# Routing logits of seven batches moved into the last batch of the first cross attention

## The chip, the cores and the metric

The kernel runs on one core of a Trainium2 chip. A core has a matrix engine (TensorE, PE in the profile, with its weight loads as PEld), a vector engine (VectorE, DVE), an activation engine (ScalarE, ACT), GpSimd (POOL) and SyncE (SP), which here only issues transfers. Each engine runs its own instruction queue in order, and queues meet at semaphores. SBUF is the working memory, PSUM the memory into which PE writes. The metric is the device time of one execution in microseconds (us); lower is better.

## What is computed

Two decoder layers over x of shape (8, 256, 256), 2048 tokens of 256 values. Each layer is: x = layernorm(x + attention(x)), x = layernorm(x + cross_attention(x, context)), x = layernorm(x + ffn(x)). The first layer's attention is windowed, its feed-forward part is a mixture of experts; the second has a gated recurrence, another cross attention and a feed-forward part with binary weights. The part around the change is this:

```python
# first cross attention: 16 heads of 16, 77 context rows per batch
scores = jnp.einsum('bhqd,bhkd->bhqk', Q, K) / np.sqrt(D_K)
...
x = _layernorm(x + _L0_xattn_ref(...))
# routing
logits = tokens @ router_w.T            # 2048 x 256 by 256 x 8
probs = jax.nn.softmax(logits, axis=-1)
top1_idx = jnp.argmax(probs, axis=-1)
top1_prob = jnp.max(probs, axis=-1)
order = jnp.lexsort((-top1_prob, top1_idx))
...
keep = jnp.zeros((T,), bool).at[order].set(keep_sorted)   # capacity 320 per expert
return jnp.where(keep, top1_idx, 0)
```

The order of tokens by probability needs the logits of all 2048 tokens, so nothing of it can start before the last token's logits are there.

## The kernel before

The stages run one after another, each in a block of its own that ends with a barrier of all engines: window attention, cross attention 0, routing and experts, recurrence, cross attention 1, binary feed-forward. The tokens stay in SBUF as `X` (the trace's `tokens`): 16 tiles of 128 tokens, two tiles per batch.

**Cross attention** (`cross_attention`, from L996) goes through 8 batches; the first and the last are written out, the six between are a loop. A batch has 8 units c = 0 to 7 of four heads each (4 units per token tile). Of a unit, PE turns the probabilities into PSUM (`turn_probs`, L1280), ACT takes their fp16 high part (`pth`, L1146), DVE the rest (`ptl`, L1186), and PE multiplies both with the values (`weigh`, L1294). ACT also makes the exponentials (L1138), POOL subtracts the maximum (L1090). The scores of two units lie in the two PSUM banks `s_banks`; from unit 5 of the last batch on nobody needs them any more. Between units stand, on two shared banks, `heads` (transposes of a tile's output `o`, L1251), ACT's copy `ot` (L1131) and `mix` (output projection, L1256), then on DVE the residual (L1203), the statistics (L145 to L150), a root on POOL (L155) and the norm's `apply` (L159), which writes the tile into `X` and counts `ln_done`. In the last batch tile 0 gets heads and mix in units 6 and 7; for tile 1 they stand in an epilogue behind unit 7, and with them a `normalise` (L1193, L1197) and the last `apply`. The queues there hold, in order:

```python
# vector                                   # tensor
both(batch)(dve)                           both(batch)(pe)
norm.apply(dve, BATCH - 1, 0, ...)         weigh(BATCH - 1, UNITS - 1, 1)
normalise(BATCH - 1, 1)                    heads, then mix (epilogue)
residual(BATCH - 1, 1, ...)
norm.apply(dve, BATCH - 1, 1, ...)
```

**Routing** (`route`, from L1371) opens by making the logits in 8 pairs of tiles, one pair per batch. Of a pair, PE turns the tokens with 4 transposes into one of two PSUM banks (L1643), ACT copies them as fp16 `xh` (L1520), DVE makes the fp16 rest `xl` (L1561), and PE makes 12 small matmuls, high x high, high x low and low x high, with 8 columns each into `l_bank` (L1471). The router's weights are loaded first in this block (L1480) and split the same way (L1515, L1557). Buffers are two, so a pair waits for the one two before it. When all are there, DVE takes `best`, the maximum per token (L1566), and `gap`; keys, ranks and slots follow (slot at L1629), then sixteen indirect DMAs by POOL write the tokens into their slots (L1508). SP issues the loads of the first experts' weights and of later stages at the start of this block (L1716 on). The experts then start with transposes of the gathered rows (L1928).

## Time and profile before

| | us |
|---|---|
| time, median of 3 runs | 1263.29 (1261.61 to 1265.4) |
| the profiled execution | 1262.5 |
| its span in the trace | 1260.8 |
| PE busy | 1073.7 (85%) |
| DVE busy | 959.5 (76%) |
| ACT busy | 692.8 (55%) |
| POOL busy | 385.3 (31%) |

The profile is one execution, taken by the hardware profiler. Its times count from the start of the span. An instruction's row gives its start, its duration, engine, line, operation and tiles; in square brackets stands how long its engine sat idle before it and what ended that. The granted clock is TensorE's, as a share of 2.4 GHz.

### The profile page before, as it was taken

How to read it: one execution, taken by the hardware profiler on the slowest of the kernel's cores; microseconds unless marked ns; L12 is line 12 of the kernel's file. 1: busy time of each engine (PE TensorE's matmuls, PEld its weight loads, DVE VectorE, ACT ScalarE, POOL GpSimd, SP SyncE). 2: the span in 40 equal slices, each digit the busy share in tenths (PEclk: the TensorE clock that was granted, in tenths of full speed). 3: DMA queues.
4: the chain of work that ended last, by engine and by line, in shares of the span. 5: the costliest groups of instructions: out<-in, count | busy, mean ns of one | idle time of the engine just before them, and what ended most of it. 6: DMA issues, size and time to landing. Idle time of an engine off the chain costs nothing. (4 is left out here: it accounts for less than half of the span.)

```text
span 1260.8 us, 30092 instructions
## 1 busy us (share of the span) xinstructions
PE 1073.7 (85%) x10763; PEld 858.9 (68%) x10763; DVE 959.5 (76%) x2126; ACT 692.8 (55%) x1459; POOL 385.3 (31%) x538
## 2 busy tenths in 40 slices
PE   5899989999998799975279999389999769998696
PEld 3578878878877577764267777377788647776485
DVE  7687878878877588984838883569998659898397
ACT  2454444444555355543637775368777725555484
POOL 5122222222221356640220000523421325665132
PEclk9899999999999899995569999699999969999799
DMA  7000000200000410007235431300000000000011
GB/s 261 7 10 2 11 12 2 83 3 2 2 2 2 162 42 22 19 1 292 74 113 176 175 117 43 123 17 18 30 12 20 1 14 23 22 11 9 35 51 50
DMA packets 34072, 65.34 MB, mean 52 GB/s; under 512 B 7591, under 2 KB 23335, under 8 KB 30887
## 3 DMA queue, kind: packets, MB, share of 16 engines
q1 hardware_dynamic: 32422, 59.62, 13.5%
q0 software_dynamic: 1536, 4.20, 1.0%
q8 instruction: 73, 1.20, 0.4%
q14 instruction: 41, 0.33, 0.1%
HBM read 43.03 MB, written 12.39 MB: 44 GB/s over the span
## 5 line engine op out<-in xcount | busy, mean ns | idle before, releaser
L1146 ACT ACTIVATE ca_pth<-ca_turned 77x512 f16<-77x512 f32 x128 | 75.9, 593 | 102.8 <-PE ca_turned L1280 102.8
L395 ACT ACTIVATE wa_probs<-wa_scores,wa_minus_top 128x192 f32<-128x192 f32 x256 | 83.3, 437 | 80.7 <-DVE wa_minus_top L488 80.7
L1090 POOL TENSOR_TENSOR ca_z<-ca_z,ca_top 128x308 f32<-128x308 f32 x128 | 88.1, 700 | 113.5 <-DVE ca_top L1181 113.4
L1186 DVE SCALAR_TENSOR_TENSOR ca_ptl<-ca_turned,ca_pth 77x512 f16<-77x512 f32 x128 | 87.1, 680 | 23.0 <-ACT ca_pth L1146 23.0
L351 POOL TENSOR_TENSOR wa_q<-wa_by_cos,wa_by_sin 128x256 f32<-128x256 f32 x32 | 23.4, 730 | 265.4 <-DVE wa_by_sin L483 265.4
L1280 PE MATMUL ca_turned<-ident,ca_probs 128*77 128x128 f32 x512 | 87.1, 294 | 15.1 <-ACT ca_probs L1138 15.0
L406 ACT ACTIVATE wa_pth<-wa_turned 128x384 f16<-128x384 f32 x128 | 58.4, 506 | 72.3 <-PE wa_turned L715 72.3
L1280 PEld LDWEIGHTS ca_turned<-ident,ca_probs 128*77 128x77 f32 x512 | 57.3, 151 | 46.0 <-ACT ca_probs L1138 26.1
L640 PE MATMUL wa_scores<-wa_xh,wa_wh 128*128 128x256 f16 x256 | 71.0, 277 | 10.1 <-DVE wa_wl L467 8.8
L488 DVE TENSOR_REDUCE wa_minus_top<-wa_scores 128x2 f32<-128x384 f32 x128 | 62.3, 548 | 20.8 <-PE wa_scores L703 18.9
L715 PE MATMUL wa_turned<-ident,wa_probs 128*128 128x128 f32 x512 | 68.3, 275 | 7.8 <-ACT wa_probs L395 3.9
L640 PE MATMUL wa_scores<-wa_xl,wa_wh 128*128 128x256 f16 x256 | 71.1, 278 | 0.0
L640 PE MATMUL wa_scores<-wa_xh,wa_wl 128*128 128x256 f16 x256 | 71.0, 277 | 0.0
L1138 ACT ACTIVATE ca_probs<-ca_z 128x308 f32<-128x308 f32 x128 | 57.7, 451 | 23.2 <-POOL ca_z L1090 23.2
L536 DVE SCALAR_TENSOR_TENSOR wa_ptl<-wa_turned,wa_pth 128x384 f16<-128x384 f32 x128 | 64.9, 548 | 6.6 <-ACT wa_pth L406 6.6
L2472 PE MATMUL re_g<-re_convh,re_w_gh 128*128 128x256 f16 x256 | 69.8, 273 | 0.0
L2472 PE MATMUL re_g<-re_convl,re_w_gh 128*128 128x256 f16 x256 | 69.8, 273 | 0.0
L2472 PE MATMUL re_g<-re_convh,re_w_gl 128*128 128x256 f16 x256 | 69.8, 273 | 0.0
L2456 PE MATMUL re_in<-re_xt,re_w_in 128*128 128x256 f32 x256 | 61.6, 402 | 9.0 <-ACT re_xt L2225 9.0
L715 PEld LDWEIGHTS wa_turned<-ident,wa_probs 128*128 128x128 f32 x512 | 57.4, 141 | 15.1 <-issue 6.2
L2456 PEld LDWEIGHTS re_in<-re_xt,re_w_in 128*128 128x128 f32 x256 | 50.9, 202 | 18.8 <-issue 7.2
L1903 DVE SCALAR_TENSOR_TENSOR ex_hl<-ex_h,ex_hh 128x320 f16<-128x320 f32 x72 | 35.2, 488 | 37.3 <-ACT ex_h L1875 36.4
(356 smaller groups left out, 3654.8 us busy)
## 6 DMA issues: line engine op xcount, KB each, us to landing
ex_stage<-in_ew SPq DMA_DIRECT2D x16, 1024.0 KB, 6.9
slots<-slots_zeros SPq DMA_DIRECT2D x10, 512.0 KB, 6.2
ca_xs<-tokens SPq DMA_DIRECT2D x16, 256.0 KB, 2.4
ex_xe<-slots SPq DMA_DIRECT2D x11, 320.0 KB, 3.2
slots<-ex_y SPq DMA_DIRECT2D x9, 320.0 KB
wa_x_stage<-in_xt SPq DMA_DIRECT2D x8, 256.0 KB, 3.1
tokens<-in_x SPq DMA_DIRECT2D x1, 2048.0 KB, 15.3
ca_w<-in_xw SPq DMA_DIRECT2D x2, 1024.0 KB, 6.6
```

What stands on the lines that cost most here:

```text
L395: ins = act.activation(probs[2 * (u % 2) + t][:, h, t * WINDOW:t * WINDOW + SPAN], s_bank[i][:, t * SPAN:(t + 1) * SPAN], ACT.Exp, bias=mi ...
L406: act.activation(spans(pth[k][:]), spans(t_bank[h][:]), ACT.Copy, scale=PSCALE).then_inc(probs_high, 1)
L488: dve.tensor_reduce(minus_top[:, g % 2, i], s_bank[i][:, 0:2 * SPAN].rearrange("p (t s) -> p t s", t=2), AX.X, ALU.max, negate=True).then_ ...
L536: dve.scalar_tensor_tensor(out=spans(ptl[k][:]), in0=spans(t_bank[h][:]), scalar=PSCALE, in1=spans(pth[k][:]), op0=ALU.mult, op1=ALU.subtr ...
L640: ins = pe.matmul(bank[:, a * SEQ:(a + 1) * SEQ], weight[:, k, cols], x[:, par, k], start=(m == 0), stop=(m == 3 * KT_ - 1))
L715: ins = pe.transpose(t_bank[h][:, j * SEQ + t * P:j * SEQ + (t + 1) * P], probs[2 * (u % 2) + t][:, h, j * P:(j + 1) * P], ident[:])
L1090: pool.tensor_tensor(z[k][:, heads], z[k][:, heads], top[:, k, heads].unsqueeze(2).broadcast_to((P, UH, CTX)), ALU.subtract).then_inc(shif ...
L1146: act.activation(pth[k][0:CTX], t_bank[k][0:CTX], ACT.Copy, scale=PSCALE).then_inc(probs_high, 1)
L1186: dve.scalar_tensor_tensor(out=ptl[k][0:CTX], in0=t_bank[k][0:CTX], scalar=PSCALE, in1=pth[k][0:CTX], op0=ALU.mult, op1=ALU.subtract).then ...
L1280: ins = pe.transpose(t_bank[k][0:CTX, h * P:(h + 1) * P], probs[k][:, h], ident[:])
L2456: ins = pe.matmul(i_bank[s % 2][:, k], w_in[:, g, m * P:(m + 1) * P], xt[:, g], start=(g == 0), stop=(g == KT_ - 1))
L2472: ins = pe.matmul(g_bank[m][:, k], w[:, j, cols], x[par][:, j], start=(n == 0), stop=(n == 3 * HT - 1))
```

## The change

The logits of pairs 0 to 6 are made inside the last batch of the first cross attention, pair 7 alone in the routing. A new class `RouteStart` holds the router's weights, the fp16 buffers, the semaphores and a table `logit` in SBUF, and tells for each engine which step stands at which place of the last batch: on PE behind units 5, 6 and 7, behind the last `weigh`, behind heads and behind mix; on ACT behind units 5, 6 and 7 and at the end; on DVE at the head of units 6 and 7's `ptl`, ahead of tile 0's apply, behind the last normalise (ahead of the last residual) and behind the last statistics (ahead of the last apply). The turned tokens go into the two banks of scores, the logits into `o_bank[0]`, the output bank of tile 0. ACT copies the logits from PSUM into `logit`, 14 tiles at the end of the attention and 2 in the routing; DVE reads them from there. The router's load stands in the attention's SP queue. The second cross attention gets a `Nothing`, whose steps are empty.

```diff
@@ cross_attention @@
+class Nothing:
...
-def cross_attention(nc, start, ctx_dram, ident, half, X, next_loads=None, table=None):
+def cross_attention(nc, start, ctx_dram, ident, half, X, follow, next_loads=None, table=None):
+        spare = [s_banks[:, UH * k:UH * (k + 1)].rearrange("p (g t) q -> p g (t q)", g=KT_) for k in range(2)]
+        turned = [bank[:].rearrange("p (g t) -> p g t", g=KT_) for bank in t_bank]
         norm = Norm(ctx, nc, tag, half)
+        follow.add_buffers(ctx, nc, tag + "next_")
         token_sum = sem("token_sum")
         scores = sem("scores")
         masked = sem("masked")
@@ -1064,6 +1089,7 @@
             start.stage(sp, X, 1, 1)
             if next_loads:
                 next_loads(sp)
+            follow.load(sp)
             if table:
                 table.fill(sp)
 
@@ -1118,6 +1144,7 @@
                 table.prepare(pool)
             both(batch)(pool)
             norm.root(pool, BATCH - 1, 1)
+            follow.gpsimd(pool, X)
 
         @block.scalar
         def _(act):
@@ -1153,11 +1180,14 @@
                         step(b + d, (par + d) % 2, kind, i, bank, uses)
                     if c == 2 and after:
                         start.value_high(act, b + 1, 1 - par)
+                    if c >= 5 and not after:
+                        follow.scalar(act, c, spare, turned, o_bank[0])
 
             power(0, 0)
             both(batch)(act)
             for kind, i, bank, uses in CA.epilogue():
                 step(BATCH - 1, 1, kind, i, bank, uses)
+            follow.scalar(act, "last", spare, turned, o_bank[0])
 
         @block.vector
         def _(dve):
@@ -1210,6 +1240,8 @@
                     if two_on and c % 2 == 0:
                         mask_scores(*two_on)
                         take_maximum(*two_on)
+                    if c >= 6 and not after:
+                        follow.vector(dve, c, spare)
                     if c == 5:
                         normalise(b, 0)
                     if c == 1 and before:
@@ -1230,11 +1262,14 @@
             mask_scores(0, 0)
             take_maximum(0, 0)
             both(batch)(dve)
+            follow.vector(dve, "applied", spare)
             norm.apply(dve, BATCH - 1, 0, at(X, (BATCH - 1) * TPB))
             normalise(BATCH - 1, 1)
+            follow.vector(dve, "normalised", spare)
             for kind, i, bank, uses in CA.epilogue():
                 if kind == "mix":
                     residual(BATCH - 1, i, bank, uses)
+            follow.vector(dve, "summed", spare)
             norm.apply(dve, BATCH - 1, 1, at(X, (BATCH - 1) * TPB + 1))
 
         @block.tensor
@@ -1309,13 +1344,19 @@
                         score_pair(b, c + 3, par)
                     if c in (5, 7) and after:
                         score_pair(b + 1, c - 5, 1 - par)
+                    if c >= 5 and not after:
+                        if c == 5:
+                            pe.wait_ge(masked, PAIRS * BATCH)
+                        follow.tensor(pe, c, X, norm, spare, turned, o_bank[0], ident)
 
             score_pair(0, 0, 0)
             score_pair(0, 2, 0)
             both(batch)(pe)
             weigh(BATCH - 1, UNITS - 1, 1)
+            follow.tensor(pe, "weighed", X, norm, spare, turned, o_bank[0], ident)
             for kind, i, bank, uses in CA.epilogue():
                 step(BATCH - 1, 1, kind, i, bank, uses)
+                follow.tensor(pe, kind, X, norm, spare, turned, o_bank[0], ident)
 
         block_scope.close()
         nc.clear_and_free_semaphores(sems + start.sems)
@@ new class, and route @@
+class RouteStart:
+    TURNS = {5: (0, 1), 6: (2,), 7: (3,), "weighed": (4,), "heads": (5,), "mix": (6,)}
+    LOGITS = {6: (0,), 7: (1,), "weighed": (2,), "heads": (3,), "mix": (4, 5, 6)}
+    HIGHS = {5: (0, 1), 6: (2,), 7: (3, 4), "last": (5, 6)}
+    LOWS = {6: (0, 1), 7: (2,), "applied": (3,), "normalised": (4, 5), "summed": (6,)}
+    EARLY = BATCH - 1
+    def __init__(self, ctx, nc, router_dram):
+        def sb(name, shape, dt=F32):
+            return ctx.enter_context(nc.sbuf_tensor("rt_" + name, shape, dt))
+        def sem(name):
+            return ctx.enter_context(nc.semaphore("rt_" + name))
+        self.router_dram = router_dram
+        self.router = sb("router", [P, KT_, EXPERTS])
+        self.router_h = sb("router_h", [P, KT_, EXPERTS], F16)
+        self.router_l = sb("router_l", [P, KT_, EXPERTS], F16)
+        self.logit = sb("logit", [P, TILES, EXPERTS])
+        self.router_loaded = sem("router_loaded")
+        self.router_high = sem("router_high")
+        self.router_low = sem("router_low")
+        self.x_turned = sem("x_turned")
+        self.x_high = sem("x_high")
+        self.x_low = sem("x_low")
+        self.logits = sem("logits")
+        self.kept = sem("logits_kept")
+    def add_buffers(self, ctx, nc, tag):
+        def sb(name):
+            return ctx.enter_context(nc.sbuf_tensor(tag + name, [P, KT_, 2 * P], F16))
+        self.xh = [sb(f"xh{k}") for k in range(2)]
+        self.xl = [sb(f"xl{k}") for k in range(2)]
+    def turn(self, pe, j, X, bank, ident):
+        if j >= 2:
+            pe.wait_ge(self.x_low, j - 1)
+        for t in range(2):
+            for g in range(KT_):
+                ins = pe.transpose(bank[:, g, t * P:(t + 1) * P], X[:, 2 * j + t, g * P:(g + 1) * P], ident[:])
+        ins.then_inc(self.x_turned, 1)
+    def multiply(self, pe, j, out, at_tile):
+        pe.wait_ge(self.x_low, j + 1)
+        pe.wait_ge(self.router_low, 1)
+        for t in range(2):
+            n = 0
+            for g in range(KT_):
+                for x, w in ((self.xh, self.router_h), (self.xh, self.router_l), (self.xl, self.router_h)):
+                    ins = pe.matmul(out[:, at_tile + t, 0:EXPERTS], x[j % 2][:, g, t * P:(t + 1) * P], w[:, g],
+                                    start=(n == 0), stop=(n == 3 * KT_ - 1))
+                    n += 1
+        ins.then_inc(self.logits, 1)
+    def high(self, act, j, bank):
+        act.wait_ge(self.x_turned, j + 1)
+        if j >= 2:
+            act.wait_ge(self.logits, j - 1)
+        act.activation(self.xh[j % 2][:], bank, ACT.Copy, scale=SCALE).then_inc(self.x_high, 1)
+    def low(self, dve, j, bank):
+        dve.wait_ge(self.x_high, j + 1)
+        dve.scalar_tensor_tensor(out=self.xl[j % 2][:], in0=bank, scalar=SCALE, in1=self.xh[j % 2][:],
+                                 op0=ALU.mult, op1=ALU.subtract).then_inc(self.x_low, 1)
+    def keep(self, act, pairs, out):
+        act.wait_ge(self.logits, pairs.stop)
+        act.activation(self.logit[:, 2 * pairs.start:2 * pairs.stop], out, ACT.Copy).then_inc(self.kept, 1)
+    def load(self, sp):
+        sp.dma_start(self.router[:], self.router_dram).then_inc(self.router_loaded, 16)
+    def gpsimd(self, pool, X):
+        pass
+    def scalar(self, act, place, spare, turned, out):
+        if place == 5:
+            act.wait_ge(self.router_loaded, 16)
+            act.activation(self.router_h[:], self.router[:], ACT.Copy, scale=SCALE).then_inc(self.router_high, 1)
+        for j in self.HIGHS.get(place, ()):
+            self.high(act, j, spare[j % 2])
+        if place == "last":
+            self.keep(act, slice(0, self.EARLY), out[:, 0:2 * self.EARLY, 0:EXPERTS])
+    def vector(self, dve, place, spare):
+        if place == 6:
+            dve.wait_ge(self.router_high, 1)
+            dve.scalar_tensor_tensor(out=self.router_l[:], in0=self.router[:], scalar=SCALE, in1=self.router_h[:],
+                                     op0=ALU.mult, op1=ALU.subtract).then_inc(self.router_low, 1)
+        for j in self.LOWS.get(place, ()):
+            self.low(dve, j, spare[j % 2])
+    def tensor(self, pe, place, X, norm, spare, turned, out, ident):
+        for j in self.LOGITS.get(place, ())[:1]:
+            if j == 0:
+                pe.wait_ge(norm.ln_done, (BATCH - 1) * TPB)
+            self.multiply(pe, j, out, 2 * j)
+        for j in self.TURNS.get(place, ()):
+            pe.wait_ge(norm.ln_done, (j + 1) * TPB)
+            self.turn(pe, j, X, spare[j % 2], ident)
+        for j in self.LOGITS.get(place, ())[1:]:
+            self.multiply(pe, j, out, 2 * j)
+def route(nc, opening, slots, ident, X, slot, starts, ahead_of_experts, binary):
 
 
     with ExitStack() as ctx:
@@ -1379,7 +1530,6 @@
         def sem(name):
             return ctx.enter_context(nc.semaphore("rt_" + name))
 
...
-        x_bank = [ctx.enter_context(nc.psum_tensor(f"rt_x{k}", [P, KT_, 2 * P], F32)) for k in range(2)]
-        l_bank = ctx.enter_context(nc.psum_tensor("rt_logit_bank", [P, TILES, 32], F32))
+        x_bank = ctx.enter_context(nc.psum_tensor("rt_x", [P, KT_, 2 * P], F32))
+        l_bank = ctx.enter_context(nc.psum_tensor("rt_logit_bank", [P, 2, 32], F32))
...
+        late = opening.EARLY
...
-            sp.dma_start(router[:], router_dram).then_inc(router_loaded, 16)
...
-            act.wait_ge(router_loaded, 16)
-            act.activation(router_h[:], router[:], ACT.Copy, scale=SCALE).then_inc(router_high, 1)
-            for j in range(TILES // 2):
-                act.wait_ge(x_turned, j + 1)
-                if j >= 2:
-                    act.wait_ge(logits, j - 1)
-                act.activation(xh[j % 2][:], x_bank[j % 2][:], ACT.Copy, scale=SCALE).then_inc(x_high, 1)
+            opening.high(act, late, x_bank[:])
+            opening.keep(act, slice(late, BATCH), l_bank[:, :, 0:EXPERTS])
             act.wait_ge(gap_ready, 1)
...
-            dve.wait_ge(router_high, 1)
-            dve.scalar_tensor_tensor(out=router_l[:], in0=router[:], scalar=SCALE, in1=router_h[:],
-                                     op0=ALU.mult, op1=ALU.subtract).then_inc(router_low, 1)
-            for j in range(TILES // 2):
-                dve.wait_ge(x_high, j + 1)
-                dve.scalar_tensor_tensor(out=xl[j % 2][:], in0=x_bank[j % 2][:], scalar=SCALE, in1=xh[j % 2][:],
-                                         op0=ALU.mult, op1=ALU.subtract).then_inc(x_low, 1)
+            opening.low(dve, late, x_bank[:])
             dve.wait_ge(consts, 13)
-            dve.wait_ge(logits, TILES // 2)
-            l = l_bank[:, :, 0:EXPERTS]
+            dve.wait_ge(opening.kept, 2)
+            l = opening.logit[:]
             then(dve.tensor_reduce(best[:], l, AX.X, ALU.max))
...
-            for j in range(TILES // 2):
-                if j >= 2:
-                    pe.wait_ge(x_low, j - 1)
-                for t in range(2):
-                    for g in range(KT_):
-                        ins = pe.transpose(x_bank[j % 2][:, g, t * P:(t + 1) * P], X[:, 2 * j + t, g * P:(g + 1) * P], ident[:])
-                ins.then_inc(x_turned, 1)
-                if j:
-                    logit(pe, j - 1)
-            logit(pe, TILES // 2 - 1)
+            opening.turn(pe, late, X, x_bank, ident)
+            opening.multiply(pe, late, l_bank, 0)
...
+        opening = RouteStart(ctx, nc, ins["router"])
-            cross_attention(nc, start0, ins["context"], ident, half, X, table=slots)
+            cross_attention(nc, start0, ins["context"], ident, half, X, opening, table=slots)
-        cross_attention(nc, start1, ins["context"], ident, half, X)
+        cross_attention(nc, start1, ins["context"], ident, half, X, Nothing())
```

## Rows read from the trace of the kernel before

**Rows 1.** The page's head: length of the profiled span.

```profile
span 1260.8 us, 30092 instructions
```

**Rows 2.** Windows: start:end, us, busy (instructions) of PE, PEld, DVE, ACT, POOL, clock, DMA share, GB/s.

```profile
560.00:565.00 5.00, 3.66 (x56) 3.09 (x56) 3.29 (x8) 2.75 (x6) 3.03 (x5) 1.00 0.01 3
565.00:570.00 5.00, 1.91 (x16) 1.36 (x15) 1.90 (x8) 0.38 (x1) 0.55 (x1) 0.73 0.00 0
570.00:575.00 5.00, 1.54 (x5) 0.77 (x4) 1.59 (x6) 0.00 (x0) 1.00 (x4) 0.50 0.00 0
575.00:580.00 5.00, 3.00 (x32) 2.54 (x31) 1.46 (x3) 1.19 (x3) 1.53 (x12) 0.50 0.74 257
580.00:585.00 5.00, 4.69 (x61) 3.67 (x58) 2.33 (x4) 2.39 (x4) 0.00 (x0) 0.50 1.01 426
585.00:590.00 5.00, 2.90 (x44) 2.10 (x42) 2.76 (x7) 1.50 (x3) 0.00 (x0) 0.50 1.01 415
...
600.00:610.00 10.00, 3.21 (x90) 2.79 (x90) 10.00 (x11) 9.90 (x8) 0.00 (x0) 0.50 0.15 59
```

**Rows 3.** Timeline: start us, us, engine, line; end of attention, opening of routing.

```profile
573.12 0.41 DVE L159 TENSOR_SCALAR tokens<-ca_res,ca_mv,ca_rstd 128x256 f32<-128x256 f32 x1 [0.66 <-POOL ca_rstd L155]
...
574.59 1.94 PE L1643 MATMUL rt_x<-ident,tokens 128*128 128x128 f32 x8 [3.46 <-PEq L1322]
...
577.05 0.22 ACT L1515 ACTIVATE rt_router_h<-rt_router 128x16 f16<-128x16 f32 x1 [8.11 <-DMA rt_router<-in_router]
...
588.94 0.29 DVE L1566 TENSOR_REDUCE rt_best<-rt_logit_bank 128x16 f32<-128x128 f32 x1 [0.65 <-PE rt_logit_bank L1471]
```

**Rows 4.** Timeline of the routing: POOL's last constant; steps of the last pair.

```profile
576.33 0.13 POOL L1502 IOTA rt_steps<- 128x7 f32 x1
...
585.84 1.09 PE L1643 MATMUL rt_x<-ident,tokens 128*128 128x128 f32 x4
...
586.97 0.60 ACT L1520 ACTIVATE rt_xh<-rt_x 128x512 f16<-128x512 f32 x1 [0.67 <-PE rt_x L1643]
...
587.60 0.69 DVE L1561 SCALAR_TENSOR_TENSOR rt_xl<-rt_x,rt_xh 128x512 f16<-128x512 f32 x1 [0.57 <-ACT rt_xh L1520]
...
588.34 0.19 PE L1471 MATMUL rt_logit_bank<-rt_router_h,rt_xh 128*128 128x8 f16 x1 [0.78 <-DVE rt_xl L1561]
...
588.66 0.17 PE L1471 MATMUL rt_logit_bank<-rt_router_h,rt_xl 128*128 128x8 f16 x1
```

**Rows 5.** Timeline of the attention: transposes at full clock, then the last batch.

```profile
518.68 0.66 PE L963 MATMUL ca_shared<-ident,ca_xs 128*128 128x128 f32 x4
...
562.43 0.69 DVE L1186 SCALAR_TENSOR_TENSOR ca_ptl<-ca_turned,ca_pth 77x512 f16<-77x512 f32 x1 [0.67 <-ACT ca_pth L1146]
...
563.30 1.03 PE L1256 MATMUL ca_shared<-ca_w,ca_ot 128*128 128x256 f32 x4
...
563.50 0.59 ACT L1146 ACTIVATE ca_pth<-ca_turned 77x512 f16<-77x512 f32 x1 [0.48 <-PE ca_turned L1280]
...
566.68 0.41 DVE L159 TENSOR_SCALAR tokens<-ca_res,ca_mv,ca_rstd 128x256 f32<-128x256 f32 x1 [0.66 <-POOL ca_rstd L155]
...
567.29 0.42 DVE L1197 TENSOR_TENSOR ca_o<-ca_out,ca_inv 128x256 f32<-128x256 f32 x1
...
567.86 0.66 PE L1251 MATMUL ca_shared<-ident,ca_o 128*128 128x128 f32 x2 [2.53 <-DVE ca_o L1197]
...
569.09 2.04 PE L1256 MATMUL ca_shared<-ca_w,ca_ot 128*128 128x256 f32 x4 [0.56 <-ACT ca_ot L1131]
...
571.17 0.42 DVE L1203 TENSOR_TENSOR ca_res<-ca_shared,ca_xb 128x256 f32<-128x256 f32 x1 [3.45 <-PE ca_shared L1256]
```

**Rows 6.** Timeline behind the routing: slots, scatter, the experts' first transposes.

```profile
619.18 0.17 DVE L1629 TENSOR_TENSOR slot<-rt_place,rt_place_side 128x16 int32<-128x16 f32 x1
...
620.34 1.24 POOL L1508 DMA_INDIRECT slots<-tokens,slot  x1 [43.73 <-DVE slot L1629]
...
648.64 1.33 PE L1928 MATMUL ex_turned<-ident,ex_xe 80*128 80x80 f32 x8 [4.94 <-DMA ex_xe<-slots]
```

More of the change, by code:

```diff
@@ L1368, in wait_filled, with add_buffers, load, gpsimd @@
         engine.wait_ge(self.zeroed, 16 * FILLS)
-def route(nc, router_dram, slots, ident, X, slot, starts, ahead_of_experts, binary):
+class RouteStart:
[22 more added lines that the diff above has]
+        self.kept = sem("logits_kept")
+    def add_buffers(self, ctx, nc, tag):
+        def sb(name):
[32 more added lines that the diff above has]
+        act.activation(self.logit[:, 2 * pairs.start:2 * pairs.stop], out, ACT.Copy).then_inc(self.kept, 1)
+    def load(self, sp):
+        sp.dma_start(self.router[:], self.router_dram).then_inc(self.router_loaded, 16)
+    def gpsimd(self, pool, X):
+        pass
+    def scalar(self, act, place, spare, turned, out):
+        if place == 5:
[5 more added lines that the diff above has]
+            self.keep(act, slice(0, self.EARLY), out[:, 0:2 * self.EARLY, 0:EXPERTS])
+    def vector(self, dve, place, spare):
+        if place == 6:
[4 more added lines that the diff above has]
+            self.low(dve, j, spare[j % 2])
+    def tensor(self, pe, place, X, norm, spare, turned, out, ident):
+        for j in self.LOGITS.get(place, ())[:1]:
[7 more added lines that the diff above has]
+            self.multiply(pe, j, out, 2 * j)
@@ L1380, in sem @@
             return ctx.enter_context(nc.semaphore("rt_" + name))
-        router = sb("router", [P, KT_, EXPERTS])
         before = sb("before", [P, P])
@@ L1392, in route @@
         plus_half = sb("plus_half", [P, 1])
-        router_h = sb("router_h", [P, KT_, EXPERTS], F16)
-        router_l = sb("router_l", [P, KT_, EXPERTS], F16)
-        xh = [sb(f"xh{k}", [P, KT_, 2 * P], F16) for k in range(2)]
-        xl = [sb(f"xl{k}", [P, KT_, 2 * P], F16) for k in range(2)]
+        opening.add_buffers(ctx, nc, "rt_late_")
         gap = sb("gap", [P, TILES, EXPERTS])
@@ L1461, in route @@
         scattered = sem("scattered")
-        def logit(pe, j):
-            pe.wait_ge(x_low, j + 1)
-            pe.wait_ge(router_low, 1)
-            for t in range(2):
-                n = 0
-                for g in range(KT_):
-                    for x, w in ((xh, router_h), (xh, router_l), (xl, router_h)):
-                        ins = pe.matmul(l_bank[:, 2 * j + t, 0:EXPERTS], x[j % 2][:, g, t * P:(t + 1) * P], w[:, g],
-                                        start=(n == 0), stop=(n == 3 * KT_ - 1))
-                        n += 1
-            ins.then_inc(logits, 1)
+        late = opening.EARLY
         block = ctx.enter_context(nc.Block())
@@ L1683, in _, with experts @@
             binary.add_sizes(pe, k_bank)
-def experts(nc, router_dram, w1_dram, w2_dram, bias_dram, slots, slot, ident, X, next_loads, gates, binary):
+def experts(nc, opening, w1_dram, w2_dram, bias_dram, slots, slot, ident, X, next_loads, gates, binary):
     with ExitStack() as ctx:
@@ L1769, in first_high2 @@
             gates.power_of_base(act)
-        route(nc, router_dram, slots, ident, X, slot, starts,
+        route(nc, opening, slots, ident, X, slot, starts,
               {"sync": first_loads, "vector": first_split, "scalar": first_high2}, binary)
@@ L2849, in ahead_loads @@
             then_loads(sp)
-        experts(nc, ins["router"], ins["ew1"], ins["ew2"], ins["eb"], slots, slot, ident, X, ahead_loads, gates, binary)
+        experts(nc, opening, ins["ew1"], ins["ew2"], ins["eb"], slots, slot, ident, X, ahead_loads, gates, binary)
         cross1 = CrossWeights(ctx, nc, "ca1", additive=True)
```

14 lines of the change are left out of this document (5 added, 9 removed).

## The prediction

> **What bounds the kernel now.** I read the page first: a span of 1260.8 us in one profiled execution of 1262.5, so 1.7 us lie outside the span [rows 1]. No engine's share decides here; the stretch between two stages does. So I went to the busy time by windows around the end of the first cross attention and the opening of the routing [rows 2]. Up to 565 the engines are busy; from 565 to 575, the epilogue of the attention, PE works 1.91 and 1.54 us of 5, DVE 1.90 and 1.59, ACT 0.38 and 0. From 575 to 590 the routing makes logits: PE is well occupied but at a granted clock of 0.50 (the 1.2 GHz level), DVE and ACT are half empty. Nothing in that stretch runs beside the logits but loads.
>
> The timeline of the opening [rows 3] gives its length. The last token tile is normalised by 573.12 + 0.41 = 573.53; the barrier takes until 574.59, when PE's first transpose starts; the first thing that needs all logits, the maximum `best`, starts at 588.94. That is 14.35 us from first transpose to `best`. ACT meanwhile waits 8.11 us for the router's weights, until 577.05, so the first two pairs of tiles are late as well.
>
> What follows `best` hangs on it in one line: the slots at 619.18, which POOL awaited for 43.73 us, sixteen indirect DMAs from 620.34, and the experts' first transposes at 648.64, which waited for the gathered rows [rows 6]. So a microsecond won at `best` should be one won at the end, unless something not moved with it becomes late.
>
> **What the change takes out of the routing.** Seven of eight pairs go, with the router's load and split. The eighth stays, and its steps are those of the last pair now [rows 4]: transposes to ACT 586.97 - 585.84 = 1.13; ACT to DVE 0.63; DVE to the first logit matmul 588.34 - 587.60 = 0.74; twelve matmuls 588.66 + 0.17 - 588.34 = 0.49; on to the next engine 588.94 - 588.83 = 0.11. New is the copy of the logits out of PSUM by ACT (128x16). The trace has no such copy; its nearest row is the router's split on ACT, 0.22 us for 128x16 [rows 3], plus some 0.03 for DVE to see it; the logit wait of 0.11 stands already in the sum. Bounds are 0 and the 0.60 of a 128x512 copy; I take 0.25. Sum 1.13 + 0.63 + 0.74 + 0.49 + 0.11 + 0.25 = 3.35 us. POOL's constants are no new limit: the last of them starts at 576.33 [rows 4], 1.74 us after the start, below 3.35. The routing becomes 14.35 - 3.35 = **11.0 us** shorter. The router's 8 KB load goes into the attention's SP queue, a batch loop earlier; there it stands ahead of the slots' zero fill and nobody waits for either.
>
> **What it puts into the last batch.** Per pair, in work: four transposes (0.66 us at full clock, 1.09 at half [rows 5, 4]), one ACT copy 0.60, one DVE subtraction 0.69, twelve matmuls 0.49. Seven pairs are 4.2 us of ACT, 4.8 of DVE, and 8 to 11 of PE. I walked the queues in program order.
>
> Units 5 and 6: eight transposes stand ahead of the turning of unit 6's probabilities, at 561.1 now; at full clock, 0.13 each (a third of 0.66 less 0.27 for the last), they free PE at about 561.6, 0.5 late. On DVE the two subtractions stand ahead of unit 6's `ptl`, which waited 0.67 us for ACT at 562.43 [rows 5]; it ends 0.7 late. Unit 7's copy, at 563.50, comes 0.65 late, and `ptl` after it. The mix of tile 0 (563.30) starts 0.65 late, and then `weigh` of unit 7 stands behind the logits of pair 1 and the transposes of pair 3.
>
> Between the batch and the epilogue: the subtraction of pair 3 stands ahead of the norm's apply at 566.68. It waits for ACT's copy of pair 3 at about 566.2 to 566.8, ends at 567.5, then come the apply and `o`, at 568.1 instead of 567.29. **First term: +0.8 us.**
>
> Epilogue: heads at 568.7 instead of 567.86. Behind them on PE now stand the logits of pair 3 and the transposes of pair 5, ahead of the mix. Only ACT's copy of the heads, 569.09 - 567.86 = 1.23 with the transposes, covers them. At half clock: 568.7 + 0.5 (heads) + 0.35 (issue of twelve matmuls, 588.34 to 588.66 [rows 4]) + 0.95 (four transposes, 1.09 less the drain of the last) = 570.5 to 570.6 against 569.09: 1.5 late, of which 0.8 was there. **Second term: +0.7.** The subtractions of pairs 4 and 5 stand ahead of the residual on DVE, but pair 5's ends near 572.0 and the mix (2.04 us at half clock [rows 5]) at 572.65, so the mix hides them; without that cover they would cost 0.7 each.
>
> After the mix: now 573.53 - 571.17 = 2.36 us from the residual to the last apply. The new chain beside it: logits of pair 4 (0.35 to issue, 0.15 of it before the mix has ended), transposes of pair 6 1.13, copy 0.63, subtraction 0.74, logits of pair 6 0.49, copy 0.11 + 0.22. From the mix's end that is 3.5 to 3.6. **Third term: +1.2.** The statistics and POOL's root run beside it.
>
> Together +2.7 at half clock. Bounds: nothing below 0, since no step of the epilogue becomes shorter at the same clock; above, see the rivals.
>
> **The clock** is the largest open point. In the trace it stands at 1.00 from 560 to 565, 0.73 on average from 565 to 570 and 0.50 after [rows 2]; PE had then done little. Heads and mix so ran at the 1.2 GHz level (0.66 and 2.04 us, against 1.03 for the mix of tile 0 [rows 5]). The added work fills those idle times, which could hold the clock up. But the same work in the routing did not raise it: 580 to 585 has PE busy 4.69 of 5 us at 0.50 [rows 2]. I take it that the clock falls where it fell.
>
> The Trainium skill bears on this (TensorE: Matmul & The Clock Gate, Part 4: PE-mode transpose): transposes do not count as a busy PE for the clock gate. The row of 580 to 585 agrees with it. Its Part 1 on what the gate does says that activity releases the throttle; by that alone the second rival's time below, 1252.7, would come.
>
> **Sum.** 11.0 - 2.7 = 8.3 us. 1262.5 - 8.3 = 1254.2; the median of the three runs is 0.8 above the profiled execution, so 1255.0. Downstream nothing is changed. The bulk loads occupy the DMA engines fully until shortly after 600 and hardly from 600 to 610 (share 0.15) [rows 2]; the slots would be ready at 611 and the scatter starts then, clear of them.
>
> **Rivals.**
> 1. *As forecast*, 1255.0, its own range 1253 to 1257: chance 0.50.
> 2. *The clock holds through the epilogue.* Heads, transposes and mix take about half: mix ends 571.0, then DVE's statistics at 572.5, subtraction of pair 6 by 573.2, logits and copy by 574.0 against 573.53: cost 0.5 instead of 2.7, 1252.7. For: PE's idle time of 2.53 us before the heads [rows 5] shrinks. Against: the 580 to 585 row. Chance 0.20.
> 3. *The clock falls earlier*, since the mix of tile 0 comes later and transposes fill the time before it. Then that mix takes 1.0 us more and the transposes of pair 3 0.43 more ahead of unit 7's `weigh`: about +1.6, cost 4.3, 1256.6. Chance 0.20.
> 4. *Slower than before.* ACT and DVE take their queues in order, so each copy and subtraction that waits for PE holds the attention's own steps. If the rounds of all seven pairs fell in series on that path, each is 1.13 + 0.63 + 0.74 + 0.49 = 2.99 us at half clock, 20.9 together against 11.0 won: +9.9, 1273. It decides from 3.7 exposed rounds on. For: steps are placed one beside another with no slack. Against: the idle time in 565 to 575 [rows 2], and my walk exposes less than one. Chance 0.03.
> 5. *Nothing is won at the end*: routing is shorter, but a load or a conversion for the experts is late. Then 1262 to 1264. Against: the loads are done 10 us before the slots, and all conversions before the experts follow the slots on DVE. Chance 0.07.
>
> **Chances and range.** A difference under 0.3% (3.8 us) is what a measurement of this kernel can't tell from none. Rivals 1 to 3 lie beyond it (0.90, 6.7 us at least); so faster 0.90, same 0.06, slower 0.04, with rival 5 leaning to same and a little to both sides. The range takes in rivals 1 to 3 and the 2 us by which the three runs stand off their median: 1250.8 to 1259.0.
>
> **What would show it.** After the change `best` starts some 3.3 us after the first transpose of the routing; that transpose starts 2.7 us later than 574.59; the second mix starts 1.5 us later; slots near 611; the experts' first transposes near 640.3. The prediction is wrong if the first transpose comes over 5 us later, if the copy of the logits takes over 1 us, or if slots and experts' transposes move by different amounts.

## The result, and the profile after the change

The changed kernel takes 1253.41 us (median of 4 runs, 1252.91 to 1253.86) against 1263.72 for the kernel before on the same chip: ratio 0.9923, 95% interval 0.9911 to 0.9936, that is 9.7 us faster (8.1 to 11.2). Its profiled span is 1251.9 us, against 1260.8 [rows 1].

The windows of the same stretch as in [rows 2], with the same columns:

```profile
560.00:565.00 5.00, 4.05 (x61) 3.75 (x62) 4.90 (x11) 3.96 (x11) 3.44 (x5) 1.00 0.01 3
565.00:570.00 5.00, 3.47 (x64) 3.05 (x63) 4.27 (x13) 2.19 (x4) 0.55 (x1) 1.00 0.00 0
570.00:575.00 5.00, 3.47 (x62) 3.08 (x61) 3.12 (x9) 1.80 (x4) 0.55 (x1) 1.00 0.02 5
575.00:580.00 5.00, 1.57 (x16) 1.12 (x16) 1.27 (x3) 0.82 (x3) 1.98 (x14) 0.55 0.58 205
580.00:585.00 5.00, 3.78 (x17) 3.41 (x17) 2.95 (x14) 2.67 (x5) 0.00 (x0) 0.50 1.01 426
```

The clock is the difference to look for. It stood at 0.73 and 0.50 from 565 to 575; now it is 1.00 in both windows, and falls at about 575.5, in the barrier. PE's busy time there went from 3.45 us to 6.94, DVE's from 3.49 to 7.39.

The end of the attention and the opening of the routing, in order of time (start, duration, engine; idle before in brackets):

```profile
569.31 0.42 DVE L1227 TENSOR_TENSOR ca_o<-ca_out,ca_inv 128x256 f32<-128x256 f32 x1
...
569.88 0.41 PE L1286 MATMUL ca_shared<-ident,ca_o 128*128 128x128 f32 x2 [1.53 <-DVE ca_o L1227]
...
570.43 0.64 PE L1454 MATMUL ca_scores<-ident,tokens 128*128 128x128 f32 x4
570.90 1.05 PE L1291 MATMUL ca_shared<-ca_w,ca_ot 128*128 128x256 f32 x4
...
572.34 0.41 DVE L1233 TENSOR_TENSOR ca_res<-ca_shared,ca_xb 128x256 f32<-128x256 f32 x1
...
573.54 0.68 DVE L1478 SCALAR_TENSOR_TENSOR ca0next_xl<-ca_scores,ca0next_xh 128x512 f16<-128x512 f32 x1
...
574.29 0.41 DVE L159 TENSOR_SCALAR tokens<-ca_res,ca_mv,ca_rstd 128x256 f32<-128x256 f32 x1
...
574.77 0.26 ACT L1484 ACTIVATE rt_logit<-ca_out 128x112 f32<-128x112 f32 x1 [1.41 <-PE ca_out L1465]
...
576.07 1.09 PE L1454 MATMUL rt_x<-ident,tokens 128*128 128x128 f32 x4 [1.34 <-PEq L1363]
...
577.20 0.60 ACT L1474 ACTIVATE rt_late_xh<-rt_x 128x512 f16<-128x512 f32 x1 [2.16 <-PE rt_x L1454]
...
579.10 0.18 ACT L1484 ACTIVATE rt_logit<-rt_logit_bank 128x16 f32<-128x16 f32 x1 [1.30 <-PE rt_logit_bank L1465]
...
579.39 0.28 DVE L1682 TENSOR_REDUCE rt_best<-rt_logit 128x16 f32<-128x128 f32 x1 [0.87 <-ACT rt_logit L1484]
```

The two transposes of the heads now take 0.41 us and the epilogue's mix 1.05; they took 0.66 and 2.04 [rows 5]. On DVE the subtraction of pair 6 (573.54) runs between statistics and apply, and ACT's copy of 14 tiles of logits is the last thing, 0.33 us behind the apply's end. The routing then has one pair; from first transpose (576.07) to `best` (579.39) are 3.32 us instead of 14.35 [rows 3].

What hangs on it, to hold against [rows 6]:

```profile
609.63 0.18 DVE L1745 TENSOR_TENSOR slot<-rt_place,rt_place_side 128x16 int32<-128x16 f32 x1
...
610.79 1.24 POOL L1635 DMA_INDIRECT slots<-tokens,slot  x1 [32.70 <-DVE slot L1745]
...
639.17 1.33 PE L2036 MATMUL ex_turned<-ident,ex_xe 80*128 80x80 f32 x8 [4.71 <-DMA ex_xe<-slots]
```

Slots and the experts' first transposes come 9.55 and 9.47 us earlier: nothing in between became late. The last batch itself began 1.3 us later in this execution than in the one before (unit 4's copy on ACT at 559.71 against 558.42), with the same code ahead of it. So positions are compared below by distances inside the stretch: **the stretch** runs from ACT's copy of unit 5's probabilities to the routing's first transpose (14.47 us before; 14.67 after, the 14.65 of the expectations being taken to PE's weight load), **the opening** from there to `best`.

### The profile page after: what moved, and what is told of

Its sections match the earlier page's. It is cut to its first block and busy times, and to the rows that moved or that the text cites. A ratio compares the mean times of both kernels' runs of the same rounds, so it can differ in the third digit from the quotient of the medians.

```text
span 1251.9 us, 30100 instructions
## 1 busy us (share of the span) xinstructions
PE 1069.3 (85%) x10763; PEld 856.2 (68%) x10763; DVE 958.7 (77%) x2126; ACT 693.1 (55%) x1461; POOL 385.7 (31%) x538
## 5 line engine op out<-in xcount | busy, mean ns | idle before, releaser
L640 PE MATMUL wa_scores<-wa_xh,wa_wh 128*128 128x256 f16 x256 | 70.4, 275 | 11.2 <-DVE wa_wl L467 9.1
```

The source lines that it names most:

```text
L640: ins = pe.matmul(bank[:, a * SEQ:(a + 1) * SEQ], weight[:, k, cols], x[:, par, k], start=(m == 0), stop=(m == 3 * KT_ - 1))
```

## Experiments

All are compared with the kernel before on the same chip. Two edits serve several of them: in "route as before" the routing has a `RouteStart` of its own with `EARLY = 0`, which loads and splits the router and makes all eight pairs, and `best` reads `l_bank` in PSUM. In the table, mix 0 is the one of tile 0, heads and mix 1 those of the epilogue. "Last fall" is the moment at which the granted clock fell to 0.50 for the rest of the attention, worked out from windows of 0.5 us and counted from the start of the epilogue's heads (minus: before them). e9 and e10 are single executions (1261.98 and 1261.31 us) and have no ratio; in e8 and e12 no transpose opens the routing, so they have no stretch and no opening.

| run | mix 0 | heads | mix 1 | last fall | stretch | opening | ratio (95%) |
|---|---|---|---|---|---|---|---|
| before | 1.03 | 0.66 | 2.04 | -0.6 | 14.47 | 14.35 | |
| after | 1.03 | 0.41 | 1.05 | +5.6 | 14.67 | 3.32 | 0.9923 (0.9911 to 0.9936) |
| e1 before again | 1.03 | 0.66 | 2.04 | -0.5 | 14.48 | 14.07 | 0.9999 (0.9988 to 1.0010) |
| e2 cost alone | 1.03 | 0.41 | 1.05 | +5.2 | 15.09 | 13.69 | 1.0001 (0.9991 to 1.0011) |
| e3 transposes only | 1.03 | 0.41 | 1.10 | +6.2 | 13.49 | 14.07 | 0.9999 (0.9990 to 1.0009) |
| e10 the same again | 1.03 | 0.41 | 2.05 | +7.3 | 14.95 | 14.05 | |
| e4 small matmuls only | 1.03 | 0.66 | 2.05 | -0.5 | 14.49 | 14.05 | 1.0011 (1.0002 to 1.0021) |
| e5 router early | 1.91 | 0.66 | 2.05 | -8.3 | 15.93 | 12.92 | 0.9998 (0.9988 to 1.0009) |
| e9 the same again | 1.03 | 0.66 | 2.05 | -0.5 | 14.50 | 12.91 | |
| e6 four pairs | 1.03 | 0.41 | 1.10 | +2.1 | 14.04 | 7.46 | 0.9951 (0.9935 to 0.9968) |
| e7 all at the end | 1.03 | 0.66 | 2.05 | -0.5 | 23.68 | 3.31 | 0.9979 (0.9969 to 0.9988) |
| e11 after again | 1.03 | 0.41 | 1.05 | +5.1 | 16.27 | 3.31 | 0.9922 (0.9910 to 0.9935) |
| e8 last pair too | 1.03 | 0.41 | 1.05 | +5.6 | | | 0.9899 (0.9882 to 0.9916) |
| e12 the same again | 1.03 | 0.41 | 1.05 | +5.2 | | | 0.9894 (0.9880 to 0.9907) |

**e1, the kernel before once more.** No edit.

> The unchanged kernel, for a second trace. The stretch asked about goes from ACT's copy of unit 5's probabilities in the last batch to the first transpose of the routing: 14.47 us before the change (560.12 to 574.59), 14.65 after it (561.40 to 576.05), though seven pairs were added. Theory A (the added PE work held TensorE's clock at 1.00 through the epilogue, which paid for the queueing): here the clock falls to 0.50 before the epilogue's mix again and the stretch is 14.5 again, give or take 0.5. Theory B (where the clock falls is chance, the trace of before caught a bad case): the stretch comes out near 13.2, with the mix near 1.03 us instead of 2.04. Ratio 1.000 under both.

PE in its epilogue:

```profile
570.63 0.66 PE L1251 MATMUL ca_shared<-ident,ca_o 128*128 128x128 f32 x2 [2.53 <-DVE ca_o L1197]
...
571.85 2.04 PE L1256 MATMUL ca_shared<-ca_w,ca_ot 128*128 128x256 f32 x4 [0.56 <-ACT ca_ot L1131]
```

The fall is no accident of the first trace: heads 0.66 and mix 2.04 again, stretch 14.48. Theory B falls for the epilogue. Where it falls, windows of the first trace show: in PE's idle time ahead of the heads, which start there at 567.86.

```profile
566.50:567.00 0.50, 0.00 (x0) 0.00 (x0) 0.32 (x1) 0.00 (x0) 0.14 (x1) 1.00 0.00 0
567.00:567.50 0.50, 0.00 (x0) 0.00 (x0) 0.47 (x3) 0.00 (x0) 0.00 (x0) 0.80 0.00 0
567.50:568.00 0.50, 0.14 (x1) 0.17 (x2) 0.21 (x1) 0.00 (x0) 0.00 (x0) 0.50 0.00 0
```

In five of the six traces without transposes ahead of the heads it is the same place, 0.5 to 0.6 us before them, though they start anywhere from 567.26 to 570.63.

**e2, the cost alone.** The attention of the changed kernel, route as before: `whole` goes to the experts in place of `opening`.

```diff
+class RouteAll(RouteStart):
+    EARLY = 0
...
-        opening = RouteStart(ctx, nc, ins["router"])
+        opening = RouteStart(ctx, nc, ins["router"], "ra_")
+        whole = RouteAll(ctx, nc, ins["router"])
```

> The seven pairs are made in the attention as after the change, and the routing makes all eight again, with a load of the router of its own, as before the change. Nothing is won, so the whole cost of the added work shows. Theory A: clock 1.00 from 565 to 575, stretch 14.7 us, kernel 0 to 0.6 us slower than before. My sum as forecast (clock falls where it fell): stretch 17.2, kernel 2.7 slower. Rival on contention later (the added work costs something further behind): over 1 us slower although the stretch is 14.7.

The stretch is 15.09, 0.62 longer than before, so seven pairs cost the attention well under the 2.7 us of my sum. Of these 0.62, 0.42 are the difference to the changed kernel's 14.67, and all of it lies ahead of `o` (8.33 us from unit 5's copy, against 7.91 there). One row there differs by as much: DVE's split of the router's weights took 0.70 us here and 0.17 in the changed kernel.

```profile
562.50 0.70 DVE L1504 SCALAR_TENSOR_TENSOR ra_router_l<-ra_router,ra_router_h 128x16 f16<-128x16 f32 x1
```

(Of the nine traces that have it in the attention, four show 0.16 or 0.17 and five 0.69 or 0.70, with both values in traces of the changed kernel; why is open.) The times don't differ (1.0001), but that doesn't make the 0.62 free: the opening is 0.66 shorter than in the trace before, since the router's weights came sooner (ACT's split starts 1.80 us behind the first transpose, 2.46 there), and the two cancel. A cost further behind of more than about 1.4 us is excluded by the interval.

**e3 and e10, only the transposes.** Route as before; of the added work PE's transposes alone (load, ACT's and DVE's steps are empty).

```diff
+class TurnsOnly(RouteStart):
...
+        for j in self.TURNS.get(place, ()):
+            pe.wait_ge(norm.ln_done, (j + 1) * TPB)
+            for t in range(2):
+                for g in range(KT_):
+                    pe.transpose(spare[j % 2][:, g, t * P:(t + 1) * P], X[:, 2 * j + t, g * P:(g + 1) * P], ident[:])
```

> The kernel before, with only the transposes of pairs 0 to 6 added on PE at their places in the last batch; no copy, no subtraction, no logits there, nobody waits for them. It tells which of the added PE work holds the clock. If transposes count as work for the clock: clock 1.00 from 565 to 572, mix 1.03 us, stretch 13.0 to 13.8 against 14.47, kernel 0.7 to 1.5 faster. If they don't: clock falls as in the kernel before, heads and mix 0.66 and 2.04 us, two times 0.95 of transposes on the path, stretch 15.3 to 16.3, kernel 1 to 2 slower.

PE in the epilogue of e3, and its window from 565 to 570:

```profile
567.36 0.41 PE L1286 MATMUL ca_shared<-ident,ca_o 128*128 128x128 f32 x2 [1.97 <-DVE ca_o L1227]
...
568.33 1.10 PE L1291 MATMUL ca_shared<-ca_w,ca_ot 128*128 128x256 f32 x4
...
565.00:570.00 5.00, 2.77 (x18) 1.96 (x16) 1.93 (x9) 0.38 (x1) 0.55 (x1) 1.00 0.00 0
```

With transposes whose results nobody reads the clock stays at 1.00, and the mix takes 1.10. The stretch is 1.0 shorter than before, inside what was expected. The ratio, 0.9999 (0.9990 to 1.0009), neither shows this 1.0 us nor excludes it; the medians are 0.9 apart (1261.92 and 1262.86). The 0.7 to 1.5 faster that I expected are so not shown in the time. In this trace the part behind the slots took 642.99 us against 641.62 and 641.93 in the two traces of the kernel before; but it took 643.15 in e9, without any transposes, so it varies by that much anyway.

> A second trace of the kernel with only the transposes added. If they hold the clock: epilogue's mix near 1.05 us and stretch near 13.5 again. If the first trace was chance: mix 2.04 and stretch 15.3 to 16.3.

```profile
565.68 0.41 PE L1286 MATMUL ca_shared<-ident,ca_o 128*128 128x128 f32 x2 [1.97 <-DVE ca_o L1227]
...
566.66 2.05 PE L1291 MATMUL ca_shared<-ca_w,ca_ot 128*128 128x256 f32 x4
```

And its windows:

```profile
565.00:566.00 1.00, 0.32 (x3) 0.35 (x4) 0.50 (x2) 0.00 (x0) 0.00 (x0) 1.00 0.00 0
566.00:567.00 1.00, 1.00 (x6) 0.72 (x5) 0.00 (x0) 0.38 (x1) 0.00 (x0) 0.59 0.00 0
567.00:569.00 2.00, 2.00 (x7) 1.54 (x7) 0.26 (x1) 0.00 (x0) 0.00 (x0) 0.50 0.00 0
569.00:570.00 1.00, 0.56 (x3) 0.16 (x1) 0.89 (x5) 0.00 (x0) 0.00 (x0) 0.71 0.00 0
570.00:573.00 3.00, 0.83 (x8) 0.86 (x8) 0.45 (x2) 0.00 (x0) 1.34 (x6) 1.00 0.00 0
```

Here the clock fell between heads and mix, and stretch 14.95 lies between the two expected values. But it isn't the fall of the kernel before: by 570 the clock was back at 1.00, with the last fall at 573. It is a **dip**, and every one of the fourteen traces has exactly one between 545 and 570, from 1.00 to 0.50 and back, while PE works. In the trace before it lay at about 553.7 to 557.1, ahead of unit 4; here it fell on the mix. Counted from the copy of unit 2, which holds the dip in both cases, to the routing's first transpose are 20.83 us in e3 (from 552.07) and 20.80 in e10 (from 551.37), against 21.68, 21.72, 21.77 and 21.82 in before, e1, e4 and e9. So the transposes made this part 0.9 us shorter both times; only where the dip lies differs.

**e4, only small matmuls.** Route as before; for each pair, at its place of logits, twelve matmuls with 8 columns and 77 rows (the real ones have 128).

```diff
+        for j in self.LOGITS.get(place, ()):
+            for n in range(12):
+                pe.matmul(spare[0][:, 0, 0:EXPERTS], self.flat[:, 0:P], self.flat[:, P:P + EXPERTS], start=True, stop=True)
```

> The kernel before, with only matmuls of the size of the logits' added on PE, twelve for each pair at the places of the logits (77 rows and 8 columns, fp16, on an operand that lies ready); no transposes, copies or subtractions. If small matmuls count as work for the clock: clock 1.00 through the epilogue, mix 1.03 us, stretch 13.2 to 13.8. If they don't: clock falls before the heads, mix 2.04 us, stretch 14.5 to 15.0, kernel 0 to 0.5 slower.

```profile
569.08 0.66 PE L1287 MATMUL ca_shared<-ident,ca_o 128*128 128x128 f32 x2 [2.23 <-DVE ca_o L1228]
...
569.53 0.51 PE L2964 MATMUL ca_scores<-ca_vh 77*128 77x8 f16 x12
...
570.30 2.05 PE L1292 MATMUL ca_shared<-ca_w,ca_ot 128*128 128x256 f32 x4 [0.27 <-ACT ca_ot L1159]
```

The twelve matmuls behind the heads are there, and yet heads and mix run at the low level. These small matmuls alone don't hold the clock; the ratio lies just above 1, that is 1.4 us slower (0.3 to 2.7) where 0 to 0.5 was expected, and since the stretch is 14.49 the trace doesn't show where. What it is about the transposes that holds it was not separated: they are longer fp32 work, and they also leave PE idle for less time ahead of the heads (1.47 to 2.03 us in the eight traces with them, 2.23 here, 2.52 to 2.55 in the other five without).

**e5 and e9, the router early.** Only load and split move; all eight pairs are in the routing (`EARLY = 0`, the four tables empty).

> Only the router's load and split are moved into the attention; all eight pairs stay in the routing. It splits the 11.0 us by which the opening of the routing became shorter. Under my account the first pair no longer waits for the load: in the kernel before, its copy starts at 577.05 though its transposes are ready 1.13 us after 574.59, so 1.3 to 1.5 us of the 11.0 are this wait and the other 9.5 are the pairs. From first transpose to the maximum: 12.9 instead of 14.35; kernel 1.4 us faster. Rival (the router's load was the larger part, pairs run fast once it is there): 2.4 us or more faster.

```profile
562.54 1.91 PE L1291 MATMUL ca_shared<-ca_w,ca_ot 128*128 128x256 f32 x4
...
568.85 2.05 PE L1291 MATMUL ca_shared<-ca_w,ca_ot 128*128 128x256 f32 x4 [0.57 <-ACT ca_ot L1158]
...
587.28 0.29 DVE L1681 TENSOR_REDUCE rt_best<-rt_logit_bank 128x16 f32<-128x128 f32 x1 [0.66 <-PE rt_logit_bank L1465]
```

The opening is 12.92, 1.43 shorter, as expected. But mix 0 took 1.91 and the stretch 15.93: the clock's last fall came at 559.4, and units 5 and 6 ran low already. That took the 1.4 back in this execution. The ratio, 0.9998 with an interval down to 0.9988, doesn't decide whether 1.4 us (0.9989) are there.

> A second trace of the kernel with the router's load and split alone in the attention. The first had the routing's opening at 12.92 us (1.43 shorter, as expected), yet its mix of tile 0 took 1.91 us and the stretch from unit 5's copy to the first transpose 15.93 instead of 14.47. Account 1 (the moment at which the clock falls moves between executions, and that one was early): this time mix of tile 0 1.03, stretch 14.5. Account 2 (the early split itself brings the fall forward): 1.9 and 15.9 again.

Mix 0 1.03, stretch 14.50, opening 12.91: account 1. When the clock falls around unit 5 changes between executions of one kernel.

**e6, four pairs.** Pairs 0 to 3 in the attention, 4 to 7 in the routing.

```diff
+    TURNS = {5: (0, 1), 6: (2,), 7: (3,)}
+    LOGITS = {6: (0,), 7: (1,), "weighed": (2,), "heads": (3,)}
+    HIGHS = {5: (0, 1), 6: (2,), 7: (3,)}
+    LOWS = {6: (0, 1), 7: (2,), "applied": (3,)}
+    EARLY = 4
```

> Pairs 0 to 3 are made in the attention, 4 to 7 in the routing. If each pair in the routing costs the pace of the trace, (587.60 - 577.78) / 7 = 1.40 us, the routing opens in 3.34 + 3 x 1.40 = 7.5 us instead of 14.35, and the kernel is 6.3 to 6.9 us faster than before, 4 less than with seven. Rival (the first pairs carry the gain): 8 or more faster. Rival (moved pairs cost the attention what they save): no more than 5 faster.

The opening takes 7.46 us against 7.5 worked out; the time is 5.1 us lower by medians, 6.2 by the ratio (4.0 to 8.2), about what was expected (6.3 to 6.9). A pair in the routing is worth its pace of 1.4 us, the first four no more than the last. The second rival's 5 us at most lies inside the interval; the trace speaks against it, since the stretch, 14.04, is no longer than before.

**e7, the same pairs, all behind the last mix.**

```diff
+        if place == "mix":
+            for j in range(self.EARLY):
+                self.turn(pe, j, X, spare[j % 2], ident)
+                if j:
+                    self.multiply(pe, j - 1, out, 2 * (j - 1))
...
+    HIGHS = {"last": tuple(range(BATCH - 1))}
+    LOWS = {"summed": tuple(range(BATCH - 1))}
```

> The same seven pairs in the same block, but all behind the last mix instead of beside units 5 to 7 and the epilogue. If the gain comes from the cover of the attention's idle engines: seven pairs at a pace of 1.2 to 1.4 us stand bare behind the mix, less the 2.36 us of residual, statistics and apply which they hide; the kernel is only 1.5 to 4 us faster than before. If moving them out of the routing is what counts, wherever they stand: 9 to 10 faster as after the change.

```profile
569.51 2.05 PE L1291 MATMUL ca_shared<-ca_w,ca_ot 128*128 128x256 f32 x4 [0.56 <-ACT ca_ot L1158]
...
571.60 0.42 DVE L1233 TENSOR_TENSOR ca_res<-ca_shared,ca_xb 128x256 f32<-128x256 f32 x1 [3.46 <-PE ca_shared L1291]
...
582.25 0.41 DVE L159 TENSOR_SCALAR tokens<-ca_res,ca_mv,ca_rstd 128x256 f32<-128x256 f32 x1
...
587.52 0.29 DVE L1678 TENSOR_REDUCE rt_best<-rt_logit 128x16 f32<-128x128 f32 x1 [0.86 <-ACT rt_logit L1482]
```

The subtractions of seven pairs stand bare between the statistics (from 571.60) and the last apply (582.25). The stretch is 9.2 longer, the opening 11.0 shorter, the ratio 0.9979, that is 2.7 us (1.5 to 3.9). Moving the pairs wins little; their cover wins. It also shows the fall again: without added work ahead of it, the mix takes 2.05.

**e11, the changed kernel once more**, beside e12.

> The changed kernel beside the next one. If the added transposes hold the clock: epilogue's mix 1.05 us, stretch 14.7 as in the first trace, routing's opening 3.3; ratio 0.992. If the first trace was a lucky one: mix 2.04, stretch near 17, ratio nearer 0.994.

PE around unit 6, and the window:

```profile
560.08 1.35 PE L1454 MATMUL ca_scores<-ident,tokens 128*128 128x128 f32 x8
...
561.22 1.06 PE L1315 MATMUL ca_turned<-ident,ca_probs 128*77 128x128 f32 x4
...
560.00:565.00 5.00, 5.00 (x58) 4.89 (x55) 3.71 (x8) 3.58 (x9) 2.51 (x4) 0.66 0.01 3
```

This time the dip lay at about 560.7 to 564.1: eight transposes took 1.35 us, those of unit 6's probabilities 1.06. The stretch is 16.27, 1.6 over the first trace; the epilogue ran at full clock all the same. In the first trace the dip lay ahead of the stretch (the window 555 to 560 is at 0.66), and unit 4 came later for it: from unit 2's copy to `best` are 25.43 us here (from 553.35) and 25.23 there (from 554.16). That fits the ratio, which is the same as in the first measurement.

**e8 and e12, the last pair too.** Pair 7 is made tile by tile at the end of the attention; the routing opens with `best`, and its wait for POOL's constants stands behind `gap`.

```diff
+    def turn_tile(self, pe, t, X, norm, bank, ident):
+        pe.wait_ge(norm.ln_done, 2 * BATCH - 1 + t)
...
-            dve.wait_ge(consts, 13)
-            dve.wait_ge(opening.kept, 2)
+            dve.wait_ge(opening.kept, 1)
```

> After the change, with pair 7 moved too: its two tiles are made one by one at the end of the attention, tile 15 alone behind the last apply and at whatever clock holds there; the routing opens with the maximum, whose wait for POOL's constants is put behind it. By rows of the trace after the change: now 3.34 us from first transpose to the maximum plus 1.35 from the last apply's end to that transpose (574.70 to 576.05) = 4.7; then two transposes 0.4, copy 0.4, subtraction 0.45, six matmuls 0.35, copy of all logits 0.3 and the barrier 1.05 = 2.95 to 3.2. 1.5 us faster than after the change, 1251.9. Rival (POOL's constants or the barrier become the bound): under 0.5 faster.

```profile
573.08 0.41 DVE L159 TENSOR_SCALAR tokens<-ca_res,ca_mv,ca_rstd 128x256 f32<-128x256 f32 x1
...
574.02 0.38 ACT L1501 ACTIVATE ca0next_xh<-ca_scores 128x256 f16<-128x256 f32 x1 [1.52 <-PE ca_scores L1485]
...
575.28 0.28 ACT L1511 ACTIVATE rt_logit<-ca_out 128x128 f32<-128x128 f32 x1 [0.88 <-PE ca_out L1493]
...
576.60 0.29 DVE L1712 TENSOR_REDUCE rt_best<-rt_logit 128x16 f32<-128x128 f32 x1 [1.74 <-PEq L1364]
```

From the last apply's end (573.49) to `best` (576.60) are 3.11 us; in the changed kernel they were 4.69. From unit 4's copy to `best` it is 18.09 against 19.68, 1.6 less, where 1.5 was expected. The time is 1249.0 us against 1251.9 expected, but on another chip; e12 was run for that.

> The kernel with pair 7 moved too, on the same chip as the changed kernel, since their first ratios (0.9899 and 0.9923) came from different jobs. By the traces it opens 1.6 us sooner (from unit 4's copy to the maximum 18.09 against 19.68 us): ratio 0.0013 lower than the changed kernel's. If the 3 us between the two ratios are real, something behind the routing gains too: 0.0024 lower.

On one chip: 1249.56 against 1252.85 us, ratios 0.9894 and 0.9922. That is 0.0028, nearer to the second expectation. The traces again show 1.6 from unit 4's copy to `best` (19.63 against 21.28, with the dip on units 5 and 6 in both), and 0.4 and 1.0 more behind `best` and behind the slots (29.89 against 30.25; 640.74 against 641.77; in e8 30.06 and 640.94). What these have to do with the edit is open. This version is faster than both kernels.

## Why the prediction came out as it did

The direction and the range held; the likeliest case did not: 1255.0 was forecast, 1253.41 measured, nearest to the second rival (clock held: 1252.7 as written, 1252.8 by its own cost of 0.5). The number alone couldn't tell the two apart, since 1253.41 lies in the first one's own range of 1253 to 1257 too; the rows on the clock do. By stretch and opening the change gains 10.8 us (28.82 to 17.99), not the 8.3 of the sum, and 9.7 (8.1 to 11.2) by the ratio.

**Opening, 11.0 us shorter: right.** 14.35 to 3.32. (e1's opening was 14.07, so single traces leave 0.3 open.) The new copy of logits takes 0.18 (0.25 with the gap was taken). e6 gives the pace of 1.4 by its own count of pairs, e5 and e9 the 1.4 of the load's wait.

**First term, +0.8: right.** From unit 5's copy to `o`: 567.29 - 560.12 = 7.17 before, 569.31 - 561.40 = 7.91 after, +0.74.

**Second term, +0.7: wrong sign.** From `o` to the last residual: 3.88 before, 572.34 - 569.31 = 3.03 after, -0.85. The queue stood as I had it, logits and transposes ahead of the mix, which starts 1.59 behind `o` instead of 1.80. But I had both at half clock, where heads, transposes and mix ran at 0.41, 0.64 and 1.05. "No step of the epilogue becomes shorter" was the bound, under the condition that the clock stays; the condition failed.

**Third term, +1.2: too large.** From the residual to the first transpose 574.59 - 571.17 = 3.42 before, 576.07 - 572.34 = 3.73 after, +0.31. Again transposes and the clock; pair 6's copy was ready at 573.37, and its subtraction stood behind DVE's statistics, which ended at 573.62. Sum of the three: 0.74 - 0.85 + 0.31 = +0.2 instead of +2.7.

**The clock: the step that failed.** I argued from the window 580 to 585, where the same kinds of work did not *raise* a clock of 0.50, that they would not *hold* one of 1.00. e3 holds it with transposes alone; e4 does not with small matmuls alone. In the six traces without added transposes ahead of the heads (before, e1, e4, e5, e7, e9) the last fall came before the heads, and heads and mix ran low; in all eight with them it came 2.1 to 7.3 us after the heads' start, heads ran at 0.41, and the mix at 1.05 to 1.10 in seven (in e10 the dip fell on it). The Trainium skill's page TensorE: Matmul & The Clock Gate, Part 4: PE-mode transpose, says of a transpose that "it doesn't count as PE-busy the same way". In e3 and e10 added transposes alone put the last fall off to 6.2 and 7.3 us behind the heads' start, so for holding the clock with these fp32 transposes the measurement decides. Why the clock stays low in the routing under the same work isn't explained by any run.

**The third rival: a low clock there does occur, but not by the cause I gave, and without its cost.** In e11 the clock was low in unit 6 and the stretch 1.6 longer. It was the dip, which lies elsewhere in other executions and costs there instead: from unit 2's copy to `best` the difference is 0.2 us (25.43 against 25.23), and the ratios are alike. In e5 it was low from unit 5 on without any pair in the attention.

**Slower, or nothing at the end:** both refuted, by the ratio and by slots and experts moving together; e2's stretch, 0.62 longer, shows that the rounds don't fall in series on the path.

## What to carry to other kernels

Work that opens a stage in a chain of small steps over four engines is worth moving into the idle engines of the stage ahead, at its measured pace per step (1.4 us here); what it costs there is decided by queue positions, and bare behind the last step it costs most of what it wins (e7: 9.2 of 11.0 us). Before costing an epilogue, look at which clock its long matmuls run: with fp32 transposes in PE's idle time the part from `o` to the residual took 2.68 us instead of 3.88 here (e3), and the whole part 0.9 less (e3, e10); the kernel's time didn't resolve so little. Distances inside a single trace move by more than a microsecond with the moment at which the clock dips, so a difference of that size needs a second trace, or a starting point ahead of the dip.

## What the runs showed of the hardware

Without added transposes the granted clock went from 1.00 to 0.50 in PE's idle time of 2.2 to 2.6 us, 0.5 to 0.6 us ahead of the epilogue's heads, in five of six traces. The transposes of the seven pairs, with nobody reading them, were enough to keep it from that fall (e3, e10). Twelve 8-column fp16 matmuls for each pair were not (e4). Besides, each of the fourteen traces has one dip to 0.50 and back, between 549 and 570, while PE works; it lay ahead of unit 4's copy in eleven of them, on units 5 and 6 in e11 and e12, on the mix in e10. What sets it off isn't known. From `best` to the slots it took 30.24 or 30.25 us in eleven of fourteen traces. What varies between executions lies ahead and behind: unit 4's copy stood between 555.52 and 561.18, the part from the slots to the end took 640.4 to 643.2.
